# A coupling network's first layer in f16 with split operands, and an end rebuilt tile by tile

## The reference

```python
def _coupling_net(h, w1, b1, w2, b2, w3, b3, w4, b4):
    h = _gelu(h @ w1 + b1)          # 256 -> 256
    h = _gelu(h @ w2 + b2)          # 256 -> 128
    h = _gelu(h @ w3 + b3)          # 128 -> 64
    return sigmoid(h @ w4 + b4)     # 64 -> 1
def _twist(x):
    o_r, o_i, p_r, p_i = split(x, 4, axis=-1)
    return concatenate([p_r, -p_i, -o_r, o_i], axis=-1)
out = x
for _ in range(3):
    tf = _coupling_net(out, ...)
    coupling = 0.1 + adaptive_range * (0.7 * gf + 0.3 * tf - 0.5) * 2.0
    out = out + coupling * _twist(out)
# around it
x = x + layernorm(attention(layernorm(x)))
x = x + layernorm(ffn(layernorm(x)))
```

## Time and profile before

| | us |
|---|---|
| median of three runs | 1103.69 |
| lowest, highest | 1103.24, 1104.42 |
| the profiled execution | 1103.25 |
| its span in the profile | 1101.4 |
| busy PE, DVE, ACT, POOL | 1008.5, 749.9, 629.3, 562.1 |
| mean granted clock of TensorE | 0.976 |

### The profile page before, as it was taken

How to read it: one execution, slowest core, us unless ns; L and a number is a source line. 1 busy time by engine, 2 the same in 40 slices (tenths; PEclk the granted TensorE clock), 3 DMA queues, 4 the chain that set the end, 5 groups by cost and what they waited for, 6 DMA issues and landing times.

```text
span 1101.4 us, 19970 instructions
## 1 busy us (share of the span) xinstructions
PE 1008.5 (92%) x7684; PEld 706.9 (64%) x7684; DVE 749.9 (68%) x1370; ACT 629.3 (57%) x1347; POOL 562.1 (51%) x690
## 2 busy tenths in 40 slices
PE   3899999999999999999999999999998889999951
PEld 1577777776777777676777676777776754433431
DVE  4868686867778696859696968696867423444465
ACT  4656565556647465656565647565655445666562
POOL 2456565445656563547484635565654422222375
PEclk9999999999999999999999999999999899999985
DMA  5200000000000000000000000000000104000015
GB/s 160 52 11 11 13 9 16 6 21 1 21 1 20 1 21 1 21 1 21 1 20 2 21 10 11 11 11 11 2 10 2 32 1 162 1 0 0 1 39 115
DMA packets 14988, 23.88 MB, mean 22 GB/s; under 512 B 5425, under 2 KB 7217, under 8 KB 14385
## 3 DMA queue, kind: packets, MB, share of 16 engines
q1 hardware_dynamic: 13964, 19.36, 6.1%
q10 hardware_dynamic: 932, 3.28, 0.9%
HBM read 13.97 MB, written 8.65 MB: 21 GB/s over the span
## 4 chain that ended last, share of the span: by engine, by line
PE 69%; DVE 19%; POOL 4%; ACT 4%; issue 2%; DMA 1%; ACTq 0%; POOLq 0%; DVEq 0%
PE ps L1150 18%; PE ps L1256 11%; PE ps L1377 7%; PE ps L1214 6%; PE ps L1191 5%; DVE arena L850 4%; PE ps L1390 3%; PE ps L1220 3%; PE ps L1201 3%; PE ps L1241 3%; PE ps L1166 3%; DVE arena L810 2%; PE ps L1228 2%; DVE arena L875 2%; DVE arena L893 2%
## 5 line engine op out<-in xcount | busy, mean ns | idle before, releaser
L1150 PE MATMUL ps<-arena 128*128 128x512 f16 x1152 | 266.4, 382 | 7.1 <-DVE arena L827 5.0
L617 ACT ACTIVATE arena<-ps,arena 128x128 f32<-128x128 f32 x512 | 139.4, 387 | 97.4 <-DVE arena L875 97.4
L1150 PEld LDWEIGHTS ps<-arena 128*128 128x128 f16 x1152 | 110.3, 98 | 127.8 <-DVE arena L827 5.4
L850 DVE STREAM_TRANSPOSE arena<-ps 128x1024 f32<-128x1024 f32 x96 | 145.6, 1516 | 24.1 <-PE ps L1150 22.2
L445 POOL TENSOR_TENSOR arena<-arena 128x256 f32<-128x256 f32 x128 | 93.4, 730 | 125.3 <-DVE arena L885 82.6
L1214 PE MATMUL ps<-arena 128*128 128x65 f32 x1024 | 136.4, 276 | 5.7 <-ACT arena L624 4.6
L1214 PEld LDWEIGHTS ps<-arena 128*128 128x128 f32 x1024 | 127.9, 193 | 18.7 <-ACT arena L624 8.1
L802 DVE BATCH_NORM_STATS2 arena<-arena 128x6 f32<-128x256 f32 x100 | 36.9, 410 | 126.5 <-ACT arena L637 121.0
L1256 PE MATMUL ps<-arena 128*128 128x256 f32 x544 | 121.9, 382 | 0.3 <-ACT arena L631 0.3
L430 POOL TENSOR_TENSOR arena<-arena 128x512 f32<-128x512 f32 x48 | 73.3, 1526 | 87.0 <-ACT arena L610 87.0
L1256 PEld LDWEIGHTS ps<-arena 128*128 128x128 f32 x544 | 102.0, 190 | 16.1 <-ACT arena L631 1.4
(11 more groups left out here) (112 smaller groups left out, 1778.3 us busy)
## 6 DMA issues: line engine op xcount, KB each, us to landing
x_rows<-arena SPq DMA_DIRECT2D x17, 256.0 KB, 2.0
arena<-x_rows SPq DMA_DIRECT2D x4, 1024.0 KB, 8.0
out_dram<-arena SPq DMA_DIRECT2D x32, 128.0 KB, 2.9
arena<-in_L_attn_x_dram SPq DMA_DIRECT2D x62, 64.0 KB
arena<-in_L_attn_Wq_dram ACTq DMA_DIRECT2D x2, 512.0 KB, 11.5
arena<-in_L_attn_Wk_dram ACTq DMA_DIRECT2D x2, 512.0 KB, 14.6
arena<-in_L_attn_Wv_dram ACTq DMA_DIRECT2D x2, 512.0 KB, 17.3
arena<-in_L_attn_Wo_dram SPq DMA_DIRECT2D x8, 128.0 KB, 4.8
```

What stands on the lines that cost most here:

```text
L617: last = act.activation(Pr[:, par, j, :], s_bank[:, par, j * P:(j + 1) * P], ACT.Exp, bias=negm[:, par, j:j + 1])
L850: dve.transpose(dst[:, d0:d0 + 32], bank.rearrange("p w (d c) -> p d w c", c=C)).then_inc(x_free, 1)
L1150: last = pe.matmul(bank[:, w, :], xc[:, lx, k, w * P:(w + 1) * P], W16[lw][:, k, i, :], start=(n == 0), stop=(n == 5))
```

## The change

1. Layer 1 of stages 4 to 11 uses f16 operands split in two, as `project` does: w1_16 (high and low part of w1) and x16 (high and low part of XT). Three f16 matmuls stand for each f32 matmul. The parts of x16 are made behind each update of stages 0 to 7: for the first half of the channels by VectorE (a copy, then a subtraction), for the second by ScalarE (a copy, `x_high`, two stages later) and GpSimd (a subtraction, `x_low`, ahead of its next update). ScalarE and VectorE make w1_16 once. The loops over the four `bb` are written out.
2. The end works by single tiles. `back` takes one tile and stands at other places: tile 0 inside stage 10, tiles 1 to 3 behind its layer 4, tiles 4 to 7 likewise in stage 11, 8 and 9 ahead of the last layer 4. Statistics, deviations and shifts get buffers for all 16 tiles; deviations and shifts are taken for groups of one to three tiles (F_GROUPS), fn has eight buffers, four of them in h1. GpSimd adds tiles 0 to 10 and waits for VectorE's last update before tile 7; VectorE adds 11 to 15.
3. The output is stored by tile, as 4 DMAs of 32 partitions each: tiles 12, 13 and 14 on ScalarE's queue behind its last normalise, all others on SP.

```diff
@@ layer 1's operands
+        w1_16 = [alloc(KT * 256 // 2, F16).rearrange("p (k n) -> p k n", k=KT) for _ in range(2)]
+        x16 = at(late_off, 2 * KT * PAIRS * NSEG * P, F16).rearrange("p (l k n) -> p l k n", l=2, k=KT)
...
+        F_GROUPS = [(0, 1), (1, 4), (4, 5), (5, 7), (7, 10), (10, 12), (12, 14), (14, 16)]
+        POOL_ADDS = 11
+        ACT_TILES = [12, 13, 14]
+        SP_TILES = [t for t in range(NT) if t not in ACT_TILES]
@@ SP
+                for t in SP_TILES:
+                    if t < POOL_ADDS:
+                        sp.wait_ge(o_done, t + 1)
+                    else:
+                        sp.wait_ge(od_done, t + 1 - POOL_ADDS)
                     for q in range(4):
-                        for y in range(2):
-                            rows = tiles[32 * q + 16 * y:32 * q + 16 * y + 16]
-                            sp.dma_start(out_rows[bp, q, y], rows).then_inc(out_st, 16)
+                        sp.dma_start(*out_tile(t, q)).then_inc(out_st, 16)
@@ GpSimd
+                def x_low(m, bb):
+                    for j in range(2):
+                        xb = XT[:, 1, bass.ds((bb * 4 + (2 * j + 1)) * 2 * P, NB)]
+                        hi, lo = (x16[:, i, 1, x16_cols(bb, j)] for i in range(2))
+                        pool.wait_ge(xb_hi, m * 2 + (j + 1))
+                        pool.tensor_tensor(lo, xb, hi, ALU.subtract).then_inc(xb_lo, 1)
...
-                for bb in range(1, PAIRS):
-                    update(bb, bb)
-                with pool.Fori(0, PAIRS) as bb:
-                    update(bb + CYCLE_M, bb)
+                for m in range(1, 2 * CYCLE_M):
+                    x_low(m - 1, (m - 1) % PAIRS)
+                    update(m, m % PAIRS)
+                x_low(2 * CYCLE_M - 1, PAIRS - 1)
                 pool.wait_ge(xr_in, 16 * PAIRS)
                 update(2 * CYCLE_M, 0)
+                f_dev(0)
+                add(0)
+                f_dev(1)
                 update(2 * CYCLE_M + 1, 1)
-                finish(0)
+                add(1)
+                f_dev(2)
+                add(2)
+                add(3)
+                add(4)
+                f_dev(3)
                 update(2 * CYCLE_M + 2, 2)
-                finish(1)
-                finish(2)
-                finish(3, 2)
+                add(5)
+                add(6)
+                f_dev(4)
+                f_dev(5)
+                pool.wait_ge(up_b, 2 * LAST_M + 2)
+                add(7)
+                f_dev(6)
+                add(8)
+                f_dev(7)
+                add(9)
+                add(10)
@@ ScalarE
+                def x_high(m, bb, j):
+                    act.wait_ge(up_b, m * 2 + (j + 1))
+                    act.activation(x16[:, 0, 1, x16_cols(bb, j)],
+                                   XT[:, 1, bass.ds((bb * 4 + (2 * j + 1)) * 2 * P, NB)],
+                                   ACT.Copy).then_inc(xb_hi, 1)
...
+                act.activation(w1_16[0], w1, ACT.Copy).then_inc(rep_done, 1)
...
+                stage(m + 2, m + 1, last=0, bb=1)
+                normalise(1)
+                normalise(2)
+                normalise(3)
+                stage(m + 3, m + 2, last=4, bb=2)
+                normalise(5)
                 layer3(LAST_M)
+                normalise(6)
                 layer4(LAST_M, PAIRS - 1)
-                for t in range(NSEG, NT):
+                for t in range(7, NT):
                     normalise(t)
+                for t in ACT_TILES:
+                    act.wait_ge(od_done, t + 1 - POOL_ADDS)
+                    for q in range(4):
+                        act.dma_start(*out_tile(t, q)).then_inc(out_st, 16)
@@ VectorE
                         dve.tensor_tensor(xa, xa, PA[j], ALU.add).then_inc(up_a, 1)
+                        if m < 2 * CYCLE_M:
+                            hi, lo = (x16[:, i, 0, x16_cols(bb, j)] for i in range(2))
+                            dve.wait_ge(up_a, m * 2 + (j + 1))
+                            dve.tensor_copy(hi, xa).then_inc(xa_hi, 1)
+                            dve.wait_ge(xa_hi, m * 2 + (j + 1))
+                            dve.tensor_tensor(lo, xa, hi, ALU.subtract).then_inc(xa_lo, 1)
@@ VectorE, the end
+                update(m + 2, 2, halves=(0,))
+                f_shift(3)
+                update(m + 2, 2, halves=(1,))
+                for t in range(7, 11):
+                    f_stats(t)
+                f_shift(4)
+                f_stats(11)
+                update(LAST_M, 3, True, (0,))
+                f_shift(5)
+                update(LAST_M, 3, True, (1,))
+                for t in range(12, 15):
+                    f_stats(t)
+                f_shift(6)
+                f_stats(15)
                 dve.wait_ge(xr_in, 16 * PAIRS)
+                add(11)
+                f_shift(7)
+                for t in range(12, NT):
+                    add(t)
@@ TensorE
+                            for lw, lx in ((0, 0), (0, 1), (1, 0)):
+                                done = pe.matmul(l1_bank[2 * j + c], w1_16[lw][:, k, c * P:(c + 1) * P],
+                                                 x16[:, lx, k, x16_cols(bb, j)], start=(n == 0), stop=(n == 5))
+                                n += 1
```

More of the change, by code:

```diff
@@ L511, in add @@
                     pool.wait_ge(fn_done, 2 * (t + 1))
[L512 to L518, removed]
+                    pool.tensor_tensor(xt, xt, fn[t], ALU.add).then_inc(o_done, 1)
                 y_dev(PAIRS - 1, NSEG)
@@ L747, in stage @@
                     layer1(m, 0)
-                    if last is not None:
-                        normalise(last)
+                    if 0 <= m - 2 < 2 * CYCLE_M:
+                        x_high(m - 2, (m - 2) % PAIRS, 0)
                     if prev is not None:
@@ L752, in stage @@
                     if last is not None:
-                        normalise(last + 1)
+                        normalise(last)
+                    if 0 <= m - 2 < 2 * CYCLE_M:
+                        x_high(m - 2, (m - 2) % PAIRS, 1)
                     if half is not None:
@@ L1035, in couple, with update @@
                     dve.wait_ge(base_done, 2 * half + 2)
-                def update(m, bb, both=False):
-                    for j in range(2):
+                def update(m, bb, both=False, halves=(0, 1)):
+                    for j in halves:
                         xa, xb = (XT[:, k, bass.ds((bb * 4 + (2 * j + 1)) * 2 * P, NB)] for k in range(2))
@@ L1368, in layer1, with back @@
-                def layer1(m, bb, j, last=None):
-                    if not (isinstance(m, int) and m < CYCLE_M):
-                        pe.wait_ge(up_a, m * 2 - 2 * CYCLE_M + (j + 1))
-                        pe.wait_ge(up_b, m * 2 - 2 * CYCLE_M + (j + 1))
+                def back(t):
+                    done = (2 * CYCLE_M + t // NSEG) * 2 + t % NSEG // 2 + 1
+                    pe.wait_ge(up_a, done)
+                    pe.wait_ge(up_b, done)
+                    if t in (1, 2, 5, 6):
+                        pe.wait_ge(l1_act, (2 * CYCLE_M + 2 + t // NSEG) * 4 + t % NSEG + 2)
+                    elif t in (3, 4, 7):
+                        pe.wait_ge(fn_done, {3: 2, 4: 8, 7: 10}[t])
+                    elif t == 10:
+                        pe.wait_ge(th_done, 2 * LAST_M)
+                    elif t in (11, 12, 13):
+                        pe.wait_ge(fn_done, 2 * (t - 5))
+                    elif t >= 14:
+                        pe.wait_ge(th_done, 2 * LAST_M + 2)
+                    for w in range(2):
+                        for k in range(KT):
+                            last = pe.transpose(back_bank(t)[:, w * D + k * P:w * D + (k + 1) * P],
+                                                XT[:, k, (2 * t + w + 2) * P:(2 * t + w + 3) * P], identf)
+                    last.then_inc(f_full, 1)
@@ L1373, in layer1 @@
+                def layer1(m, bb, j, last=None):
+                    if m >= CYCLE_M:
+                        if m == CYCLE_M:
+                            pe.wait_ge(w1_lo, 1)
+                        pe.wait_ge(xa_lo, m * 2 - 2 * CYCLE_M + (j + 1))
+                        pe.wait_ge(xb_lo, m * 2 - 2 * CYCLE_M + (j + 1))
                     for c in range(2):
-                        if last is not None and j == 1:
-                            pe.wait_ge(fn_done, 2 * (last + c + 1))
+                        if last is not None and j == 1 and last > 0:
+                            pe.wait_ge(fn_done, 2 * (last - 2 + c))
+                        n = 0
@@ L1417, in stage @@
                     layer1(m, bb, 0)
+                    if last is not None:
+                        back(last)
                     if prev is not None:
@@ L1425, in stage @@
                     if prev is not None:
-                        layer4(prev, last)
+                        layer4(prev)
+                    if last is not None:
+                        for t in range(last + 1, last + 4):
+                            back(t)
                     layer2(m)
```

(2 more changed lines are left out.)

156 lines of the change are left out of this document (73 added, 83 removed).

## The result

| | before | after |
|---|---|---|
| median, us | 1103.47 | 1127.43 |
| lowest to highest | 1102.35 to 1104.42 | 1125.5 to 1128.88 |
| profiled execution, its span | 1103.25, 1101.4 | 1127.71, 1125.9 |
| mean granted clock | 0.976 | 0.959 |

The changed kernel takes 1.0216 times as long as before, 95% interval 1.0198 to 1.0235. The forecast was 1086.1 us, faster by 1.6%. Sign and size are wrong.

A forecast was written before the change was run, and what follows sets the result against it. TensorE was taken to bound the stages. From the median 1103.69 us: -10.1 (six f16 stages) - 12.0 (end) + 3.3 (first update) + 1.2 (clock) = -17.6, giving 1086.1 us, range 1082 to 1091.

The forecast's parts named there:

- The end, last transfer and landing: Behind the last add: last transfer issued at 58.6 us after layer 1 of stage 10, landing 3.2, span's end at 61.9.
- One of the prediction's own signs: At the end: prediction wrong if one queue's last issue is more than 2 us behind the other's.
- the one on the other side: Rival for a slower kernel: GpSimd's low part takes 2.9 us or more, 1107.3 us at 3.1; chance 0.02.
- The end, last add: Last add ends 53.0 us after layer 1 of stage 10, before 66.6; its row takes 11.0 in place of 17.8.
- VectorE's last update: In the end: it finishes 42.0 us after layer 1 of stage 10, where it was 48.8 before.
- The first mark: Layer 1 of stage 11 starts 12.84 us after layer 1 of stage 10, where it was 14.35 before.
- Layer 1 in f16: Stages 4 to 11: a half takes 2.59 us for 3.43, a stage 11.08 for 12.76; stages 4 to 9 win 10.1.
- The shared queue: VectorE and GpSimd work added as one queue: 10.7 of 11.08 us a stage, fits; rival that it bounds, chance 0.14.
- The first update: Stage 0: added split delays the last rows' transposes by 3.3 us, with TensorE idle for 4.1.
- The clock: Behind TensorE's idle time at the last rows, a stretch at half clock costs 1.2 us, bounds 0 and 2.9.
- ScalarE's issues: In the end: ScalarE issues 12 stores at 0.61 us each, ending 0.3 us before SP.
- the rival of 0.94: ScalarE issues slowly, 0.94 us a store, its 12 stores end 4.0 us later: 1089.7 us; chance 0.06.

The follow-up runs named there:

- e1: The changed kernel with each store cut in two at y, so 8 stores of 16 partitions per tile, 128 in all: 1096.22 us, ratio to before 0.9917.
- e3: The kernel before with only its stores changed to 64 of 32 partitions and one tile each, all on SP: 1144.58 us, ratio to before 1.0362.
- e4: The changed kernel with the stores of all tiles except tile 0 going to a scratch tensor, 32 rows outermost: 1087.96 us, ratio to before 0.9836.
- e12: The changed kernel with 48 grouped stores of 16 partitions, and VectorE's split of the first update moved behind the last rows' statistics: 1090.32 us, ratio to before 0.9858.
- e11: Repeat of e2, run in the same job as e12: 1094.95 us, ratio to before 0.9908.
- e2: The changed kernel with stores of 16 partitions and several tiles in one, 48 in all: 1092.91 us, ratio to before 0.9877.
- e7: The kernel of e12 with tiles 8 to 11 in 8 stores, and the last four tiles as 3 stores on SP, 5 on ScalarE: 1087.93 us, ratio to before 0.9842.

## Why the prediction was wrong, step by step

- *The end, last transfer and landing.* This is the step that failed. It took 0.61 us an issue and "the landing as before (3.2 us...)", so it priced a store by its issue and never by its bytes and the number of engines that carry them. Between the last add and the end of the span I had 8.9 us; it is 45.4: 36.5 of the 42 us by which the forecast's span (1083.8) was short. The rest is the last add (2.8), the clock (1.5) and the attention part (1.4), below. The cause is the outermost dimension of 2, as e1, e3 and e4 show from three sides. One of the prediction's own signs came with it: SP's last issue starts 20.2 us behind ScalarE's (1114.8 and 1094.6). My question on the x loads was only how long their issue takes; the share beside them, 0.10, would have told. 82 us of transfer do not fit into an end of 62 us. No rival had it either: the one on the other side was GpSimd's low part, which took 1.34 us.
- *The end, last add.* A smaller term that was also short. Forecast 53.0, found 55.8 (1024.61 to 1080.45). VectorE's last update ends at 43.9 for 42.0, and the row behind it takes 11.9 for 11.0. The timeline of VectorE and GpSimd in after shows where:

```profile
1071.76 1.26 POOL L542 TENSOR_TENSOR arena<-arena 128x512 f32<-128x512 f32 x1
1071.82 1.22 DVE L1128 SCALAR_TENSOR_TENSOR arena<-arena 128x4 f32<-128x4 f32 x1 [0.48 <-POOL arena L537]
...
1075.70 3.00 POOL L542 TENSOR_TENSOR arena<-arena 128x512 f32<-128x512 f32 x2
1075.76 1.22 DVE L1128 SCALAR_TENSOR_TENSOR arena<-arena 128x4 f32<-128x4 f32 x1 [1.19 <-POOL arena L537]
1076.90 3.55 DVE L1134 TENSOR_TENSOR arena<-arena 128x512 f32<-128x512 f32 x4
```

  A shift of 128x4, 0.16 us where nothing is beside it, takes 1.22 twice, because GpSimd's add began 0.06 us before: 2.1 us. The last four adds take 3.55 us where I counted 4 x 0.60: 1.15 us. I had counted such waits in the stages and left them out here. Together they are more than the 0.9 us; what took the rest back I haven't taken apart. Two more shifts took 1.22 and 1.23 us ahead of VectorE's last update (at 1046.08 and 1053.80); that they are its 1.9 us is likely and not shown. The first mark, layer 1 of stage 11, was written down as 12.84, where 14.35 less 1.68 is 12.67; it was found at 12.7.
- *Layer 1 in f16.* Right: a half 2.59 us, a stage 10.98 for 11.08. One stage in six lost 0.5 us to layer 3's activation.
- *The shared queue.* Right that it fits. I had 0.3 to 0.6 us for the copy. All sixteen copies start while GpSimd's update of the same half runs, and take 1.37 to 1.38; each ends 0.3 us behind that update, so what it adds to the shared queue is near the lower bound. GpSimd's low part takes 1.34 (forecast 1.3):

```profile
980.94 1.77 POOL L520 TENSOR_TENSOR arena<-arena 128x512 f32<-128x512 f32 x1 [2.07 <-DVE arena L1105]
981.62 1.38 DVE L1111 CAST arena<-arena 128x512 f16<-128x512 f32 x1
```

  TensorE is busy 10.98 of 10.98 us.
- *The first update.* Right: from layer 1 of stage 0 to the transposes it is 35.90 us before and 39.04 after, 3.1 us for the forecast 3.3, behind 3.96 us of idle TensorE (forecast 4.1).
- *The clock.* Right that it falls, but too small: forecast 1.2, found 2.7 (transposes 1.11 for 0.66, the eight passes 5.69 for 3.43 us). I had taken 3.6 us at the lower level, half of it idle. The stretches of after around the transposes (928.55) have it at a mean of 0.75 and then of 0.60:

```profile
925.30:929.30 4.00, 0.74 (x4) 0.75 (x5) 2.06 (x8) 0.02 (x1) 0.90 (x2) 0.75 1.01 428
929.50:935.30 5.80, 5.80 (x10) 2.18 (x10) 0.86 (x2) 1.28 (x2) 0.00 (x0) 0.60 0.50 212
```

  With levels of 0.5 and 1 that is 2.0 us and 4.6 us at the lower one, and only some 1.2 us of it lie ahead of the transposes.

- *ScalarE's issues.* The first six take 0.61 to 0.68 us, forecast 0.61, and in e4 0.44 at the median: nothing speaks for the rival of 0.94.

From the attention part 1.4 us more came, with no change in it (layer 1 of stage 0 at 889.51 for 888.12); over the kernels here, none of which touches that part, the mark lay between 887 and 893 us.

## What to carry to other kernels

Price a DMA twice, by its issue and by its bytes over the engines that carry it, and read the outermost dimension of both sides for the second. A loop that merges two dimensions into one transfer to halve the number of DMAs may leave two engines of sixteen; here the rate fell from some 200 GB/s to 51. When a transfer pattern stands somewhere in the trace already, read the DMA share and GB/s there, also where other work hides it: two of sixteen engines is 0.13. And work moved ahead of a point where TensorE stands waiting is paid twice, once as the wait and once as the clock behind it; behind that point nothing of it showed in the time (e12 against e11).

## What the runs showed of the hardware

- With 2 outermost, two packets of 2 KB were in flight at a time, 84 ns each, and moved 51 GB/s, whether one queue issued or two; stores with 16 outermost moved up to 241 GB/s in the kernel before.
- From start to start an issue takes 0.46 us for a store of 16 partitions and one tile (32 KB, e1), 0.46 for two tiles (64 KB, e2's last eight) and 0.57 for four (128 KB, before), so larger stores give an issuing queue more rate: 71, 141 and, worked out the same way, 229 GB/s. With the transfers in the way it takes 1.4 for four (e7).
- The issue of 64 KB in 32 partitions takes 0.67 us from start to start with 2 outermost (the changed kernel, while nothing holds it up) and 0.46 with 32 outermost (e4).
- A small operation of VectorE suffers from GpSimd as much as a large one: 0.16 us became 1.22 beside an add that had begun 0.06 us before.
- Behind 3.96 us without work the granted clock was 0.60 from 929.5 to 935.3 us, in the profiled execution. In e11 the eight passes behind 3.96 us without work took 5.54 us, in e12 behind 0.82 us 3.44.
